# A four-stage mixer network on one core: constant products at four more places of TensorE's order, and the depthwise taps prepared later

## The chip, the cores and the metric

The kernel runs on 1 core of one Trainium2 chip. The metric is the device time of one execution in microseconds (us). Engines are named as the profile names them: PE is TensorE (matmuls), PEld its weight loads, DVE VectorE, ACT ScalarE, POOL GpSimd, SP the queue that issues the DMAs.

## The reference, cut to what matters

The input `x` is 16 images of 64 channels and 16 by 16 pixels, in single precision: 4096 tokens of 64 channels. Four stages follow one another, each a "conv" part and an "ffn" part with a residual:

```
x = x + _L0_conv_ref(_ln_c(x), ...)   # normed pixels -> 3x3 conv to 32 clusters, softmax, pooled, small MLP
t = t + _L0_ffn_ref(_ln_t(t), ...)    # router picks 127 of each image's 256 tokens, FFN 64->256->64
x = x + _L1_conv_ref(_ln_c(x), ...)   # four band means, argmax, two small products, sigmoid gate per image and channel
t = t + _L1_ffn_ref(_ln_t(t), ...)    # 16 experts 64->128->64, top 2, computed densely
x = x + _L2_conv_ref(_ln_c(x), ...)   # 3x3 depthwise conv, then linear attention with 8 heads
t = t + _L2_ffn_ref(_ln_t(t), ...)    # 8 experts 64->256->64, top 2, computed densely
x = x + _L3_conv_ref(_ln_c(x), ...)   # 3x3 conv 64->64 with weights quantised to 4 bits
t = t + _L3_ffn_ref(_ln_t(t), ...)    # 8 experts 64->128->64, the top 2 of each image
```

The comments are mine. In the first conv part the pixels are centred, scaled to unit length and convolved:

```
xn = l2norm(feature, axis=1)
sa = jax.nn.softmax(conv2d(xn, conv_up_w, conv_up_b, 1), axis=1)
```

In the second one the input is multiplied by a sigmoid gate `s` (`return x * s[:, :, None, None]`) that follows from band means through an argmax and two small products. The third one begins with `kdw = lax.conv_general_dilated(fmap, wdw, ..., feature_group_count=C)`: nine taps per channel.

## The kernel before

The whole of `x` stays on the chip. Tokens lie on the 128 partitions, in 32 tiles of 64 channels (`X`). The work goes through in G = 4 groups of 8 tiles (`TG`), or in 8 chunks of 512 tokens (`NCHUNK`). Each engine has one list of instructions, written out by hand at the end of `build`: for PE the order is `xt_tensor`, `w0_tensor`, `c0_tensor`, `u_tensor`, `t_tensor`, `f_tensor`, `v_tensor`, `e1_tensor`, `d_tensor` and so on, and for DVE `c0_vector`, `u_vector`, `t_vector`, `f_weights`, `f_vector`, `v_vector`, `e1_vector`, `d_vector`. An engine runs its list strictly in that order; between engines there are only semaphores (`wait_ge`, `then_inc`). What stands earlier in a list therefore delays all that stands behind it on that engine.

`keep_clock(pe, bank, count, tile)` (L421) issues `count` products of a constant 128 by 128 tile with itself into a PSUM bank that nobody reads; in single precision each shows as two MATMUL records. It stands in many gaps of PE's list.

The places that the change touches, in order of time:

- `w0_tensor` (L444) transposes the small weights of the first stage and then issues 6 constant products. Behind it, `c0_tensor` (L752) transposes the first group's unit-length pixels as soon as DVE has made them (L766, DVE L686); ACT copies them into the padded image (L722); the first convolution (`conv`, L784) is 72 records of 64 by 32 weights. After each convolution come two constant products and then the transposes of the logits (L799).
- `f_tensor` (L1174) is the first FFN. Its last loop turn, g == G, only transposes the last group's output back (`back`, L1242), which waits until DVE has consumed an earlier one (`f_yb`).
- `v_tensor` (L1351) computes band means (L1369), each group behind 6 constant products and a wait for the normed tokens, then 6 more constant products (L1373), the product for the argmax (L1374), the transposes of later weights (`prep_tensor`), 4 constant products, two small products (L1381, L1383), and last the gates: 16 products of 64 rows with a broadcast weight (L1388), a semaphore after every fourth.
- `e1_tensor` (L1783) begins with a wait for the second gated group (`x3`), 18 constant products, and then the transposes of group 0 (L609), which wait for DVE's `split` (L603, L604).
- DVE's `v_vector` (L1299) begins with `prep_taps` (L1643): two copies of the identity (L1648), four small instructions, and 18 `tensor_scalar` of 128x64 that place nine taps in a high and a low part (L1654, L1655). Behind them DVE copies the band means (L1307) that PE's L1374 waits for. After the argmax and `hq` (L1322) come `prep_vector` and `e1_weights_vector` (L1547), and then the gates' use (L1332). The taps are read only by the depthwise convolution in `d_tensor` (L2101).
- `e1_vector` (L1689) runs 16 experts over each chunk. For each expert e: `gate` (L1712) multiplies two hidden halves; PE's hidden products of expert e + 2 wait for it. At e % 4 == 3 two pair sums are weighed (`weigh`, L1717), which POOL adds up (L1500); the last two pairs of a chunk are weighed in the next chunk at e == 3, and PE transposes the finished sum at e == 6 (`experts_back`, L1589). At e == 7 and 8 the sum is reduced and added to X, at e == 9 to 13 the next layer norm's statistics are taken.

## Time and profile before

| | us |
|---|---|
| median of 3 runs | 706.9 |
| lowest, highest of the runs | 706.47, 711.89 |
| the profiled execution's own time | 704.68 |
| its span, first to last instruction | 702.9 |
| PE busy in it | 623.2 (89%) |
| DVE, ACT, POOL busy | 450.8, 364.4, 260.5 |
| mean granted clock of PE | 0.949 |

A clock of 1.00 is full speed, 0.50 the lower of the two levels. PE's busy time contains the constant products, so it says nothing by itself about what bounds the kernel; the chain of waits does. Times within the span count from its first instruction.

### The profile page before, as it was taken

How to read it: one execution, taken by the hardware profiler on the slowest of the kernel's cores; microseconds unless marked ns; L12 is line 12 of the kernel's file. 1: busy time of each engine (PE TensorE's matmuls, PEld its weight loads, DVE VectorE, ACT ScalarE, POOL GpSimd, SP SyncE). 2: the span in 40 equal slices, each digit the busy share in tenths (PEclk: the TensorE clock that was granted, in tenths of full speed). 3: DMA queues.
4: the chain of work that ended last, by engine and by line, in shares of the span. 5: the costliest groups of instructions: out<-in, count | busy, mean ns of one | idle time of the engine just before them, and what ended most of it. 6: DMA issues, size and time to landing. Idle time of an engine off the chain costs nothing.

```text
span 702.9 us, 12272 instructions
## 1 busy us (share of the span) xinstructions
PE 623.2 (89%) x3776; PEld 412.3 (59%) x3776; DVE 450.8 (64%) x1323; ACT 364.4 (52%) x777; POOL 260.5 (37%) x349
## 2 busy tenths in 40 slices
PE   7887788886999999999998998998999999996784
PEld 5675437774555555555556776895545445465652
DVE  6555797878777787778776477565433333438566
ACT  3234586176544444444436454455666777435375
POOL 6402555250653543444353000270333333335153
PEclk8999998798999999999999899989999999999897
DMA  4900000204343433524301000022222222100001
GB/s 110 159 6 1 2 0 1 61 2 101 87 112 76 97 83 68 113 61 112 68 9 30 1 2 0 1 51 52 77 70 80 60 61 61 31 2 0 2 2 60
DMA packets 24532, 34.62 MB, mean 49 GB/s; under 512 B 10984, under 2 KB 20224, under 8 KB 22368
## 3 DMA queue, kind: packets, MB, share of 16 engines
q1 hardware_dynamic: 24480, 33.95, 20.8%
q8 instruction: 30, 0.49, 0.3%
q14 instruction: 22, 0.18, 0.1%
HBM read 32.50 MB, written 1.44 MB: 48 GB/s over the span
## 4 chain that ended last, share of the span: by engine, by line
PE 61%; DVE 24%; ACT 6%; issue 4%; POOL 3%; DMA 1%; DVEq 1%; ACTq 0%; SPq 0%; POOLq 0%
PE ps L1808 13%; PE ps L2384 9%; PE ps L2400 8%; PE ps L1828 6%; DVE ST L492 3%; PE ps L2506 2%; PE ps L426 2%; PE ps L784 2%; PE ps L609 1%; PE ps L2782 1%; PE ps L1589 1%; PE ps L2111 1%; PE ps L2089 1%; PE ps L2113 1%; DVE tk L1106 1%
## 5 line engine op out<-in xcount | busy, mean ns | idle before, releaser
L1500 POOL TENSOR_TENSOR out_acc<-out_acc,tok_tmp 128x512 f32<-128x512 f32 x80 | 103.6, 1295 | 211.3 <-DVE tok_tmp L1717 114.7
L1808 PE MATMUL ps<-tokT,w 128*128 128x512 f32 x512 | 134.5, 409 | 3.4 <-DVE hid_buf L1712 1.9
L1769 ACT ACTIVATE act_buf<-ps 128x512 f32<-128x512 f32 x128 | 75.8, 596 | 92.0 <-PE ps L1808 88.4
L1808 PEld LDWEIGHTS ps<-tokT,w 128*128 128x128 f32 x512 | 92.6, 190 | 52.6 <-issue 24.3
L2384 PE MATMUL ps<-tokT,w 128*128 128x512 f32 x256 | 67.7, 406 | 1.5 <-ACT hid_buf L2357 1.5
L2384 PEld LDWEIGHTS ps<-tokT,w 128*128 128x128 f32 x256 | 45.4, 188 | 28.4 <-ACT hid_buf L2357 13.9
L426 PE MATMUL ps<-ones 128*128 128x128 f32 x416 | 58.4, 294 | 1.4 <-DVE X L1005 1.4
L1712 DVE TENSOR_TENSOR hid_buf<-act_buf,ps 128x512 f32<-128x512 f32 x64 | 43.5, 685 | 19.9 <-ACT act_buf L1769 16.3
L426 PEld LDWEIGHTS ps<-ones 128*128 128x128 f32 x416 | 53.6, 206 | 3.9 <-DVE X L1005 1.7
L1712 DVE TENSOR_TENSOR tok_split<-act_buf,ps 128x512 f32<-128x512 f32 x64 | 43.4, 686 | 15.7 <-ACT act_buf L1769 14.7
L537 ACT ACTIVATE U<-X,nmr,rstd 128x64 f32<-128x64 f32 x104 | 36.5, 430 | 23.4 <-POOL nmr L515 18.3
L2357 ACT ACTIVATE hid_buf<-ps,b 128x512 f32<-128x512 f32 x64 | 38.5, 682 | 17.3 <-PE ps L2384 17.3
L2357 ACT ACTIVATE tok_split<-ps,b 128x512 f32<-128x512 f32 x64 | 38.8, 690 | 13.1 <-PE ps L2384 12.8
L2313 DVE SCALAR_TENSOR_TENSOR tok_tmp<-ps,b,disp_all 128x512 f32<-128x512 f32 x24 | 18.0, 752 | 42.8 <-PE ps L2400 42.5
L1717 DVE TENSOR_TENSOR tok_tmp<-ps,disp_all 128x512 f32<-128x512 f32 x56 | 37.3, 688 | 6.4 <-PE ps L1828 3.5
L575 ACT ACTIVATE U<-X,nmr,rstd (+1 forms) x64 | 23.0, 430 | 25.6 <-POOL nmr L568 25.6
L514 POOL TENSOR_TENSOR rstd<-vpe,neghalf 128x8 f32<-128x8 f32 x20 | 34.4, 1721 | 1.7
L512 POOL TENSOR_TENSOR nmean<-mean2x,neghalf 128x8 f32<-128x8 f32 x20 | 4.7, 233 | 74.5 <-DVE var L499 74.3
L1828 PE MATMUL ps<-tok_split,w 128*64 128x512 f32 x128 | 31.0, 605 | 0.4 <-DVE tok_tmp L1717 0.4
L1828 PE MATMUL ps<-hid_buf,w 128*64 128x512 f32 x128 | 31.0, 605 | 0.0
L2400 PE MATMUL ps<-hid_buf,w 128*64 128x512 f32 x128 | 31.0, 605 | 0.0
L2400 PE MATMUL ps<-tok_split,w 128*64 128x512 f32 x128 | 30.9, 604 | 0.0
(475 smaller groups left out, 1133.7 us busy)
## 6 DMA issues: line engine op xcount, KB each, us to landing
disp_all<-disp_dram SPq DMA_DIRECT2D x32, 512.0 KB, 6.1
disp_all<-disp_dram SPq DMA_DIRECT2D x32, 256.0 KB, 3.9
w_raw<-in_L_ffn_w SPq DMA_DIRECT2D x4, 512.0 KB, 7.8
XIN<-in_x SPq DMA_DIRECT2D x4, 256.0 KB, 3.8
w_raw<-in_L_ffn_W SPq DMA_DIRECT2D x2, 512.0 KB, 5.8
out<-XIN SPq DMA_DIRECT2D x4, 256.0 KB, 2.2
fc_raw<-in_L_conv_upfc_w SPq DMA_DIRECT2D x1, 512.0 KB, 4.6
w<-in_L_ffn_w SPq DMA_DIRECT2D x1, 512.0 KB, 11.6
```

What stands on the lines that cost most here:

```text
L426: pe.matmul(ps[:, bank, 0:P], tile[:, :], tile[:, :], start=True, stop=True)
L514: plink(pool.tensor_tensor(rstd[:, t0:t1_], vpe[:, t0:t1_], neghalf[:, t0:t1_], ALU.pow))
L537: last = act.activation(U[:, tt, :] if dst is None else dst[:, t, :], src[:, tt, :], ACT.Identity, bias=nmr[:, tt:tt + 1], scale=rstd[:, t ...
L1500: pool.tensor_tensor(out_acc[:, :], out_acc[:, :], weighed[p % 2], ALU.add).then_inc(mm["acc"].sem, 1)
L1712: dve.tensor_tensor(hid_buf[e % 8][:, :], act_buf[e % 2][:, :], ps[:, 2 + e % 2, :], ALU.mult).then_inc(mm["m1"].sem, 1)
L1717: dve.tensor_tensor(out_acc[:, :] if p == 0 else weighed[p % 2], ps[:, 4 + p % 2, :], disp_all[:, p // 4, p % 4, :], ALU.mult).then_inc(mm ...
L1769: act.activation(act_buf[e % 2][:, :], ps[:, e % 2, :], ACT.Silu).then_inc(mm["act"].sem, 1)
L1808: last = pe.matmul(ps[:, 2 * k + e % 2, :], w12[:, part, k, EXPERT1[e], :], tokT[:, bass.ts(i, CHUNK)], start=(part == 0), stop=(part == 1))
L1828: last = pe.matmul(ps[f * C:(f + 1) * C, 4 + p % 2, :], w3[:, EXPERT1[e], :], hid_buf[e % 8][:, :], start=True, stop=True)
L2357: act.activation(hid_buf[u % 8][:, :], ps[:, u % 4, :], ACT.Gelu, bias=b1_6[:, unit:unit + 1]).then_inc(mm["act"].sem, 1)
L2384: last = pe.matmul(ps[:, u % 4, :], w1_6[:, part, e, h * P:(h + 1) * P], tokT[:, bass.ts(i, CHUNK)], start=(part == 0), stop=(part == 1))
L2400: last = pe.matmul(ps[r * C:(r + 1) * C, 4 + p % 2, :], w2_6[:, EXPERT2[u], h, :], hid_buf[u % 8][:, :], start=(h == 0), stop=(h == 1))
```

## The change

Five edits. (1) The constant products behind the first stage's weight transposes go from 6 to 11. (2) Two constant products are issued between the unit transposes and the first group's convolution. (3) In the last turn of the first FFN's loop PE waits for the last GELU (`f_h`) and issues 8 constant products into bank 3, ahead of the last `back`. (4) Behind each of the four groups of gates stand 3 constant products. (5) `prep_taps` leaves the head of `v_vector`; its six small instructions run in the experts' second chunk (`chunk(1, 0)`) at e == 3, ahead of `weigh`, and the 18 `tensor_scalar` are dealt out there as two behind each of the experts 4 to 12 (`place_tap`). In the added turn the code says `e == 3` and `4 <= e < 13`; nothing else in that chunk changes.

```diff
--- before.py
+++ after.py
@@ -454,7 +454,7 @@
             pe.transpose(ps[0:C, 1, C:2 * C], t1_raw[:, C:2 * C], ident[0:C, 0:C])
             pe.transpose(ps[0:C, 1, 2 * C:3 * C], t2_raw[:, :], ident[0:C, 0:C])
             pe.transpose(ps[0:C, 1, 3 * C:3 * C + K0], cent_raw[:, :], ident[0:K0, 0:K0]).then_inc(s_t[0], 1)
-            keep_clock(pe, 2, 6, ident)
+            keep_clock(pe, 2, 11, ident)
 
         def fc_tensor(pe):
 
@@ -769,6 +769,8 @@
             def conv(g):
 
                 xp = padded_pair[g % 2][:, :, :].rearrange("p q (y x) -> p q y x", x=PADW)
+                if g == 0:
+                    keep_clock(pe, 2, 2, ident)
                 pe.wait_ge(*m["c0_xp"](g + 1))
                 if g >= 1:
                     pe.wait_ge(*m["c0_cv"](g))
@@ -1255,6 +1257,9 @@
                     last.then_inc(m["f_mt_ps"].sem, 1)
                 if g < G:
                     outp(g)
+                if g == G:
+                    pe.wait_ge(*m["f_h"](2 * NCHUNK))
+                    keep_clock(pe, 3, 8)
                 if g >= 1:
                     back(g - 1)
 
@@ -1298,7 +1303,6 @@
 
         def v_vector(dve):
 
-            prep_taps(dve)
             dve.wait_ge(*m["v_w_ps"](1))
             dve.tensor_copy(l1w1T[:, :], ps[0:C, 7, 64:96])
             dve.tensor_copy(l1w2T[:, :], ps[0:C // 2, 7, 128:192]).then_inc(m["v_w"].sem, 1)
@@ -1389,6 +1393,7 @@
                                  ident[0:C, 0:C], start=True, stop=True)
                 if b % BG == BG - 1:
                     last.then_inc(m["v_sb_ps"].sem, 1)
+                    keep_clock(pe, 3, 3)
 
 
         def router_tensor(pe, g, w2, ne, bank, done):
@@ -1650,9 +1655,11 @@
             vlink(dve.tensor_copy(gw2_6[:, 0, :], gw_6[:, :]))
             dve.tensor_tensor(gw2_6[:, 1, :], gw_6[:, :], gw2_6[:, 0, :].bitcast(F32), ALU.subtract)
             vlink(dve.tensor_tensor(dw_lo[:, :], dw_raw[:, :], dw_hi[:, :].bitcast(F32), ALU.subtract))
-            for t in range(9):
-                dve.tensor_scalar(wdw[:, t, 0, :], ident2[:, :], dw_hi[:, t:t + 1].bitcast(F32), None, ALU.mult)
-                dve.tensor_scalar(wdw[:, t, 1, :], ident2[:, :], dw_lo[:, t:t + 1], None, ALU.mult)
+
+        def place_tap(dve, t):
+
+            dve.tensor_scalar(wdw[:, t, 0, :], ident2[:, :], dw_hi[:, t:t + 1].bitcast(F32), None, ALU.mult)
+            dve.tensor_scalar(wdw[:, t, 1, :], ident2[:, :], dw_lo[:, t:t + 1], None, ALU.mult)
 
         def prep_vector(dve):
 
@@ -1717,7 +1724,7 @@
                 dve.tensor_tensor(out_acc[:, :] if p == 0 else weighed[p % 2], ps[:, 4 + p % 2, :],
                                   disp_all[:, p // 4, p % 4, :], ALU.mult).then_inc(mm["w"].sem, 1)
 
-            def chunk(i, prev):
+            def chunk(i, prev, taps=False):
                 for e in range(E1):
                     gate(i, e)
                     if prev is not None:
@@ -1729,6 +1736,11 @@
                             dve.wait_ge(*mm["x"](prev + 1))
                         for step in STEPS_AT.get(e, ()):
                             chunk_stats(dve, prev, X, m["d_var"], step)
+                    if taps:
+                        if e == 3:
+                            prep_taps(dve)
+                        elif 4 <= e < 13:
+                            place_tap(dve, e - 4)
                     if e % 4 == 3:
                         for p in (e // 2 - 3, e // 2 - 2):
                             if p >= 0:
@@ -1738,7 +1750,7 @@
                     if prev is None:
                         router_top2(dve, mm, route1, 1, E1, e)
             chunk(0, None)
-            chunk(1, 0)
+            chunk(1, 0, taps=True)
             with vchain.loop(2, NCHUNK, 3) as i:
                 chunk(i, i - 1)
             for p in (PAIRS1 - 2, PAIRS1 - 1):
```

## Rows read from the trace of the kernel before

**Rows 1.** The page's span, and PE's clock in 40 slices

```profile
span 702.9 us, 12272 instructions
...
PEclk8999998798999999999999899989999999999897
```

**Rows 2.** Busy time by stretch, 12 to 22 us: length, five engines, clock, DMA share, GB/s

```profile
12.00:14.00 2.00, 0.67 (x6) 0.44 (x6) 1.93 (x13) 0.60 (x1) 2.00 (x1) 0.80 0.30 63
...
20.00:22.00 2.00, 1.31 (x31) 0.95 (x37) 1.54 (x3) 0.60 (x1) 0.51 (x1) 1.00 0.11 20
```

**Rows 3.** Instructions of PE by time, 1.5 to 24 us: start, us, what, idle before

```profile
1.57 2.50 PE L426 MATMUL ps<-ident 128*128 128x128 f32 x10 [1.57 <-POOL ident L408]
...
8.82 1.60 PE L426 MATMUL ps<-ident 128*128 128x128 f32 x12
12.55 0.66 PE L766 MATMUL ps<-ident,unit 128*128 128x128 f32 x4 [2.13 <-DVE unit L686]
13.99 4.49 PE L784 MATMUL ps<-padded_pair,w_cu_t 64*32 64x256 f32 x72 [0.78 <-ACT padded_pair L722]
...
21.48 2.36 PE L784 MATMUL ps<-padded_pair,w_cu_t 64*32 64x256 f32 x72 [0.69 <-ACT padded_pair L722]
```

**Rows 4.** The same of PE, behind the first FFN

```profile
107.06 1.09 PE L1242 MATMUL ps<-ident,ffn_outT 128*128 128x128 f32 x4 [2.91 <-DVE XIN L1117]
...
108.48 2.93 PE L426 MATMUL ps<-ones 128*128 128x128 f32 x12
```

**Rows 5.** Instructions of DVE by time: the last group of the FFN, and the taps

```profile
112.96 0.69 DVE L1117 TENSOR_TENSOR XIN<-ps,wm 128x512 f32<-128x512 f32 x1
...
120.62 0.39 DVE L1648 COPY ident<-ident 64x64 f32<-64x64 f32 x2 [0.61 <-ACT U L537]
...
121.58 0.25 DVE L1654 TENSOR_SCALAR wdw<-ident,dw_hi 128x64 fp32r<-128x64 f32 x1
...
124.35 0.25 DVE L1655 TENSOR_SCALAR wdw<-ident,dw_lo 128x64 fp32r<-128x64 f32 x1
...
124.74 0.20 DVE L1307 COPY ori<-ps 64x64 f32<-64x64 f32 x1
```

**Rows 6.** Instructions of PE by time, band means to the experts' transposes

```profile
121.97 1.60 PE L426 MATMUL ps<-ones 128*128 128x128 f32 x12
125.00 0.33 PE L1374 MATMUL ps<-ori,wencb 64*64 64x64 f32 x2 [1.42 <-DVE ori L1307]
...
129.24 7.08 PE L1388 MATMUL ps<-ident,sg 64*128 64x64 f32 x32 [0.27 <-ACT sg L1347]
136.25 5.81 PE L426 MATMUL ps<-ones 128*128 128x128 f32 x36
142.80 1.09 PE L609 MATMUL ps<-ident,tok_split 128*128 128x128 f32 x8 [0.74 <-DVE tok_split L604]
```

**Rows 7.** Busy time by stretch, where the gates begin

```profile
129.00:129.50 0.50, 0.26 (x1) 0.27 (x2) 0.49 (x3) 0.18 (x1) 0.00 (x0) 0.74 0.00 0
```

**Rows 8.** Instructions of DVE by time, around the first gated group

```profile
130.95 0.18 DVE L1547 TENSOR_TENSOR gw<-gw,gw 128x16 fp32r<-128x16 f32 x1
131.24 0.69 DVE L1332 TENSOR_TENSOR tok_tmp<-U,ps 128x512 f32<-128x512 f32 x1
...
134.60 0.69 DVE L1332 TENSOR_TENSOR tok_tmp<-U,ps 128x512 f32<-128x512 f32 x1
```

**Rows 9.** Instructions of DVE in the second chunk, behind expert 3, and at 8 and 12

```profile
191.38 0.69 DVE L1717 TENSOR_TENSOR tok_tmp<-ps,disp_all 128x512 f32<-128x512 f32 x1 [0.16 <-PE ps L1828]
...
200.25 0.69 DVE L1712 TENSOR_TENSOR hid_buf<-act_buf,ps 128x512 f32<-128x512 f32 x1 [0.52 <-ACT act_buf L1769]
...
206.04 0.69 DVE L1712 TENSOR_TENSOR tok_split<-act_buf,ps 128x512 f32<-128x512 f32 x1 [0.37 <-ACT act_buf L1769]
```

**Rows 10.** PE in the second chunk: the sum's transposes

```profile
195.45 0.66 PE L1589 MATMUL ps<-ident,out_acc 128*128 128x128 f32 x4 [0.26 <-POOL out_acc L1500]
```

**Rows 11.** ACT at the second chunk's end: the norm of the first chunk's tokens

```profile
209.96 1.44 ACT L575 ACTIVATE U<-X,nmr,rstd 128x64 f32<-128x64 f32 x4 [1.16 <-POOL nmr L568]
```

## The prediction

> **What bounds the kernel now.** The page's span and clock line come first [rows 1]: 702.9 us, of which two slices of 17.6 us stand at 0.7 of the clock; everywhere else it is nearly full. The chain of waits then says who sets the end where the change acts: from 12 to 24 us it runs over PE, ACT and DVE in turn, with the first convolution whole in it; from 102 to 147 us it is nearly all DVE, with short pieces of PE; from 170 us on it is PE in the experts. The order by time and the busy time by stretch give the prices.
>
> In the first stage PE waits 2.13 us for DVE's unit pixels and 0.78 us for ACT's copy [rows 3]. In that gap the granted clock falls: 0.80 over 12 to 14 us (full, then half), and 1.00 again from 20 us [rows 2]. The same 72 records take 4.49 us for the first group and 2.36 us for the second [rows 3]. Behind the FFN PE is idle for 2.91 us while DVE works [rows 4]. At 120.62 DVE starts on the taps and at 124.74 it copies the band means; PE has long finished its constant products and waits 1.42 us for that copy [rows 5, 6]. The gates run at half clock, 7.08 us for 32 records [rows 6, 7], though DVE takes each group when it comes to it. In the second chunk PE waits only 0.26 us for the sum [rows 10], and DVE has little left over [rows 9].
>
> **The prices of a constant product.** Twelve records (six products) took 1.60 us at full clock [rows 3, 6] and 2.93 us at half clock [rows 4]: 0.27 and 0.49 us a product.
>
> **Edits 1 and 2, the first convolution.** Five more products end at 10.42 + 1.35 = 11.8 us, before the unit transposes at 12.55; two more fit between the transposes' end (13.21) and the convolution (13.99): 0.54 us of 0.78. At full clock both cost nothing, since DVE and then ACT end those waits. At half clock the second pair would cost 0.98 - 0.78 = 0.2 us and the first five up to 11 x 0.49 - (12.55 - 8.82) = 1.7 us. The first ten records of the span took 2.50 us, the slow price, so the clock begins low, and the twelve from 8.82 took the fast one [rows 3]. The idle time left is 0.75 + 0.24 us instead of 2.13 + 0.78. If the clock stays up, the convolution takes 2.36 instead of 4.49 us (2.1 us), and the products and transposes behind it, at two levels in the rows of this stretch, give another 0.3 us. PE, ACT and DVE of groups 1 to 3 follow from that, and POOL's powers are ready ahead of them, so I take 2.4 us as kept to the end. Bounds: 0 (the clock falls all the same, or had not fallen) to 2.4.
>
> **Edit 3, behind the FFN.** The wait asks for the count that the last `outp`, ahead of it in PE's list, has waited for already, so it is free; queued behind it are the last `back` and the small transposes of `v_tensor`, which nobody waits for yet. Eight products are 2.1 us at full clock, inside the 2.91 us gap; at half clock 3.9 us, 1.0 too many. But DVE takes that `back` only at 112.96 [rows 5], 4.8 us after it ended [rows 4], so cover remains either way. DVE, POOL and ACT set the end until 120.5; PE's speed from 105 to 112 us gives back nothing. Price 0, bounds 0 to 0.
>
> **Edit 5, what it removes.** The 24 instructions stand from 120.62 to about 124.5 us, the 18 `tensor_scalar` (the first and the last are shown) 0.163 us apart [rows 5]. Without them the copy can run at 122.1, when the last band product is done. But PE has six constant products in its order ahead of L1374; they end at 121.97 + 1.60 = 123.57 [rows 6]. So L1374 moves from 125.00 to about 123.5: 1.5 us gained, not 3.9. All behind it (argmax, gates, X) moves with it.
>
> **Edit 5, what it adds.** At expert 3 of the second chunk the six small instructions take 121.58 - 120.62 = 0.96 us [rows 5], in front of the weighing at 191.38, for which DVE had been free for 0.16 us [rows 9]: 0.8 us later. POOL's last two sums follow, and PE, which already waits for them [rows 10], starts the transposes 0.8 us later. Behind the experts 8 to 11 four pairs cost 4 x 0.326 = 1.30 us on a DVE that from 200.25 to 206.04 shows 0.37 us of idle time [rows 9]; gate 12 comes 0.9 us late at most, and PE's second product of expert 14 waits for that gate. The last statistics and POOL's power come as much later, and then ACT's four norms, which already end a wait of 1.16 us and stand ahead of the third chunk's first Silu [rows 11]. PE has a few tenths in hand at each. Bounds 0 to 0.9 + 0.9 = 1.8 us, taken 0.85, the middle, since PE's double buffers take some of it once. Together 1.65 us. The pairs behind 4 to 7 fall into waits for ACT like that of 0.52 us ahead of gate 8 [rows 9] and cost nothing; if that cover were gone they would add 1.3 us. The taps' reader stands a whole stage further on, so nobody waits for them.
>
> **Edit 4, the gates.** At full clock a group of gates would come after 1.0 instead of 2.0 us. But DVE is in its own list until 131.13 and takes the first group at 131.24 [rows 8]: 0.1 us to gain. DVE takes the second group 3.36 us after the first [rows 8]; with three products each the groups come every 2.0 + 1.2 = 3.2 us at half clock, every 1.8 us at full clock. Then 18 products stand ahead of the transposes L609.
>
> **Sum**, against the profiled execution's own 704.68 us: - 2.4 - 1.5 - 0.1 + 1.65 = - 2.35, thus 702.3. The median of the runs lies 2.2 us above that execution, and I carry this over: 704.5 us.
>
> **Rival A: the convolution's clock is not there to be won.** In the gap before L784 the clock fell in this execution; one execution cannot say that it always does, and the runs of this one program spread from 706.47 to 711.89. If it had not fallen in the timed runs, or falls still, edits 1 and 2 give 0: 706.9 + 0.05 = 706.9. The Trainium skill (TensorE: Matmul & The Clock Gate, Part 1) says that the gate's look at PE is not tied to the kernel's start and that the transition varies from run to run. By that rule A would hold in part of the executions; the sum above takes the fall as seen. No row of one execution can show it.
>
> **Rival B: slower, by the gates.** The clock falls where the gates begin, as it did at 129 us [rows 7]. With a thin mixture of gates and constants it stays at 0.50 through all four groups: 7.08 us, plus 24 records x 0.24 = 5.9, thus 13.0 us, and then the 18 products, which took 5.81 us in part at half clock [rows 6]. From 127.7 that ends at 146.5 us, where DVE's split has been ready since about 141.3 (142.8 - 1.5): 5.2 us late, straight on the path. This decides once the clock is still low when the third group ends. The total would be 706.9 - 2.35 + 5.2 = 709.8. For it: the clock stayed at 0.50 for all 32 records before. Against it: constants at half clock brought it up within the row of 36 that followed.
>
> **Rival C: the taps are free.** PE hides the whole of edit 5's addition, as its short waits in the second chunk allow [rows 10]: 704.5 - 1.65 = 702.9.
>
> **How the numbers follow.** Forecast 0.37; A 0.33; B 0.15; C 0.12; 0.03 for something else. The likeliest gives 704.5 us. With 0.6 us for other executions on both sides, the range from C's 702.9 less that and some of the unshown to B's lower part is 701.8 to 708.8; it leaves out the upper half of B and little below. About 1% (7 us) is what a measurement of this kernel can tell from no change. Faster than 699.8 would need every bound and more: 0.04. Slower than 714.0 would need B and a second wait: 0.03. The rest, 0.93, is the same.
>
> **What would show it.** Right: the first convolution's 72 records in 2.4 us; L1374 about 1.5 us after the last band product, with no wait for DVE; the transposes L1589 of the second chunk behind a wait of about 1 us; a gap of some tenths on PE near the third chunk's start. Wrong: half clock in that convolution (A), constants of the gates still running when DVE's first split is done (B), no longer waits of PE in the second chunk (C). A range missed below would mean that the clock was low in places that this trace shows high.

## The result: slower by 0.9%, where no change was forecast

The changed kernel took 713.41 us (median of 20 runs, 706.59 to 718.49), the kernel before 706.36 us on the same chips (20 runs, 702.05 to 711.89). The ratio is 1.0088, 95% interval 1.0064 to 1.0112. The forecast was 704.5 us, 701.8 to 708.8. Ratios here and below leave out runs over 1.5% above the fastest of the same kernel; where that matters, the mean of all runs is given beside it.

The profiled execution of the changed kernel took 715.96 us, that of before 704.68 us: 11.3 us to explain. The page has the span, and PE's clock in slices of 17.9 us. Two slices stand at 0.6 now, from 107 to 143 us, where there was a 0.7 and a 0.8 [rows 1].

```profile
span 714.2 us, 12380 instructions
...
PEclk9998996688999999999999899968999999999997
```

The first convolution came as forecast. In the order by time (start, duration, what, idle before and its releaser) its 72 records take 2.36 us instead of 4.49 us [rows 3]; the products ahead of it end in time.

```profile
13.98 2.36 PE L786 MATMUL ps<-padded_pair,w_cu_t 64*32 64x256 f32 x72 [0.34 <-ACT padded_pair L722]
```

Behind the FFN it goes wrong. The same view, 102 to 127 us:

```profile
102.35 1.95 PE L426 MATMUL ps<-ones 128*128 128x128 f32 x16
105.42 0.63 PE L1244 MATMUL ps<-ident,ffn_outT 128*128 128x128 f32 x4 [1.13 <-DVE XIN L1119]
...
106.29 1.60 PE L426 MATMUL ps<-ones 128*128 128x128 f32 x12
110.02 1.39 PE L1373 MATMUL ps<-band,U 128*64 128x4 f32 x16 [2.13 <-ACT U L537]
111.33 2.93 PE L426 MATMUL ps<-ones 128*128 128x128 f32 x12
114.19 1.87 PE L1373 MATMUL ps<-band,U 128*64 128x4 f32 x16
115.99 2.93 PE L426 MATMUL ps<-ones 128*128 128x128 f32 x12
...
120.65 2.93 PE L426 MATMUL ps<-ones 128*128 128x128 f32 x12
...
126.41 0.32 PE L1378 MATMUL ps<-ori,wencb 64*64 64x64 f32 x2
```

With edit 3's eight products at 102.35 the clock is full here, and everything after them is over early: the six constants at 106.29 take 1.60 us where before they took 2.93 us [rows 4]. PE then idles for 2.13 us, and while the first band means run the clock falls. From there each group costs 4.66 us (111.33 to 115.99 to 120.65): six constants at half clock and 16 records of band means at half clock. ACT delivers a group every 3.4 us, so no group waits any more and PE falls behind. The encoder's product L1378 stands at 126.41; without its taps DVE does nothing but wait for it:

```profile
124.98 0.22 DVE L1311 COPY ori<-ps 64x64 f32<-64x64 f32 x1 [5.78 <-PE ps L1373]
```

At the gates (order by time of PE, then of DVE):

```profile
130.65 1.57 PE L1392 MATMUL ps<-ident,sg 64*128 64x64 f32 x8 [0.27 <-ACT sg L1351]
132.15 1.65 PE L426 MATMUL ps<-ones 128*128 128x128 f32 x6
133.73 1.97 PE L1392 MATMUL ps<-ident,sg 64*128 64x64 f32 x8
...
140.67 1.97 PE L1392 MATMUL ps<-ident,sg 64*128 64x64 f32 x8
142.57 7.61 PE L426 MATMUL ps<-ones 128*128 128x128 f32 x42
150.02 1.04 PE L609 MATMUL ps<-ident,tok_split 128*128 128x128 f32 x8
```

```profile
143.10 0.72 DVE L604 TENSOR_TENSOR tok_split<-U,tok_split 128x512 fp32r<-128x512 f32 x1
```

DVE's split is ready at 143.82 us, PE comes to it at 150.02: 6.2 us late, behind 21 constants in a row. The busy time by stretch (length, five engines, clock, DMA share, GB/s) shows the three long stretches at half clock. PE had no idle time in any of them:

```profile
111.00:124.00 13.00, 13.00 (x77) 12.28 (x76) 4.72 (x23) 7.83 (x21) 4.62 (x8) 0.50 0.00 0
132.00:148.00 16.00, 16.00 (x69) 14.86 (x69) 14.97 (x67) 5.52 (x16) 8.11 (x15) 0.50 0.33 66
470.00:486.00 16.00, 16.00 (x76) 15.65 (x75) 6.35 (x27) 6.84 (x15) 8.62 (x11) 0.50 0.29 55
```

The third lies in the second experts' router, code that the change doesn't touch. Before, half clock lasted there from 463.7 to 470.5 us. In the second chunk, DVE's weighing comes at 198.00 (191.38 [rows 9]) and ACT's norm at 218.38 (209.96 [rows 11]); the six small instructions stand ahead of the first, and a pair of `tensor_scalar` behind each expert. Two of these pairs, the ones behind the experts 4 and 8, fall together with work of POOL and take much longer than the others (DVE's order by time, with POOL's row beside it):

```profile
198.00 1.29 DVE L1724 TENSOR_TENSOR tok_tmp<-ps,disp_all 128x512 f32<-128x512 f32 x2
...
200.75 1.31 DVE L1662 TENSOR_SCALAR wdw<-ident,dw_lo 128x64 fp32r<-128x64 f32 x1
...
208.25 0.72 DVE L1661 TENSOR_SCALAR wdw<-ident,dw_hi 128x64 fp32r<-128x64 f32 x1
```

```profile
208.01 0.91 POOL L1582 TENSOR_TENSOR w<-w_whole,w 128x256 fp32r<-128x256 f32 x1
```

```profile
218.38 1.44 ACT L575 ACTIVATE U<-X,nmr,rstd 128x64 f32<-128x64 f32 x4 [1.80 <-POOL nmr L568]
```

**Where the 11.3 us arose in this execution**, by starts against those of before: L1378 +1.4, L609 +7.2, the first weighing of the second chunk +5.9 (174.09 to 179.96; part of PE's lateness meets waits that were there), ACT's norm +8.4. The half clock of 17 instead of 7 us in the later router brings 4.4 more, and a shorter stretch near 670 us takes 1.5 back.

### The profile page after: what moved, and what is told of

Read it like the earlier page. It is cut to its first block, busy times and chain, and to the rows that moved or that the text cites. A ratio compares the mean times of both kernels' runs of the same rounds, so it can differ in the third digit from the quotient of the medians.

```text
span 714.2 us, 12380 instructions
## 1 busy us (share of the span) xinstructions
PE 639.6 (90%) x3830; PEld 429.1 (60%) x3830; DVE 452.0 (63%) x1323; ACT 364.3 (51%) x777; POOL 260.3 (36%) x349
## 3 DMA queue, kind: packets, MB, share of 16 engines
q1 hardware_dynamic: 24480, 33.95, 20.4%
## 4 chain that ended last, share of the span: by engine, by line
PE 48%; DVE 13%; ACT 3%; issue 3%; POOL 2%; DVEq 1%; ACTq 0%; POOLq 0%
PE ps L1820 11%; PE ps L2396 8%; PE ps L2412 8%; PE ps L1840 5%; PE ps L2518 2%; DVE ST L492 1%; PE ps L609 1%; PE ps L2123 1%; PE ps L2101 1%; PE ps L1594 1%; PE ps L2125 1%; PE ps L2113 1%; PE ps L2144 1%; PE ps L2794 1%; DVE U L592 1%
## 5 line engine op out<-in xcount | busy, mean ns | idle before, releaser
L426 PE MATMUL ps<-ones 128*128 128x128 f32 x456 | 71.2, 315 | 0.8 <-DVE X L1007 0.8
L426 PEld LDWEIGHTS ps<-ones 128*128 128x128 f32 x456 | 65.2, 225 | 3.6 <-DVE X L1007 1.1
```

What stands on the lines that cost most here:

```text
L426: pe.matmul(ps[:, bank, 0:P], tile[:, :], tile[:, :], start=True, stop=True)
```

## The experiments

Each was run 12 times unless said otherwise, those of one group on one chip together with the kernel before. The theory: constants in PE's fixed order cost what they take at half clock wherever PE has no wait left to put them in; this happens at the band means and at the gates. The rivals: edit 5's addition costs it, or the clock falls by chance alone. A ratio has an interval of about 0.3% to either side, so the difference of two ratios is known to about 0.4%.

**First group: each edit alone** (before: 706.88 us). Edit 5 alone, the taps moved and nothing else:

```diff
-            prep_taps(dve)
...
-            chunk(1, 0)
+            chunk(1, 0, taps=True)
```

> Edit 5 alone: the taps leave the head of v_vector and go into the experts' second chunk; no constant product is added. Theory 1 (constant products in PE's fixed order decide): the profile shows 2.5 us more between the second chunk's expert 3 and the third chunk's start, as in the changed kernel, and 0 to 1.5 us less at L1374, because six constant products stand ahead of it; time +1.0 to +2.5 us against before. Theory 2 (the chunk's DVE work is the main cost): +4 us or more.

Measured 708.93 us, ratio 1.0025 [0.9994, 1.0055]. The trace has both halves. The encoder's product stands at 122.48, 2.5 us earlier than before; 1.0 of this was there already at the last `back` (106.03, 107.06 before [rows 4]), where edit 5 has not acted yet, so the taps' removal gave 1.5 us. And the distance to before, -2.8 us at the second chunk's start, is -0.3 us at its end.

```profile
106.03 1.00 PE L1242 MATMUL ps<-ident,ffn_outT 128*128 128x128 f32 x4 [2.91 <-DVE XIN L1117]
...
122.48 0.33 PE L1373 MATMUL ps<-ori,wencb 64*64 64x64 f32 x2
```

Edit 4 alone:

```diff
                     last.then_inc(m["v_sb_ps"].sem, 1)
+                    keep_clock(pe, 3, 3)
```

> Edit 4 alone: three constant products behind each group of gates. Theory 1: where the clock is low at the gates it stays low through all four groups, PE's list is 24 records of 0.22 us = 5.3 us longer there, 0.7 us of it covered, and the first transposes L609 come 4 to 5 us late, straight on the path: +3 to +5 us, the largest of the single edits. Theory 2: the clock is up sooner and the products lie in PE's spare time: 0 us, -1 at best.

Measured 710.16 us, ratio 1.0055 [1.0028, 1.0081]. The order by time of PE has the 21 constants and the late transposes, with the band means undisturbed:

```profile
140.47 6.34 PE L426 MATMUL ps<-ones 128*128 128x128 f32 x42
146.65 1.04 PE L609 MATMUL ps<-ident,tok_split 128*128 128x128 f32 x8
```

Edit 3 alone:

```diff
+                if g == G:
+                    pe.wait_ge(*m["f_h"](2 * NCHUNK))
+                    keep_clock(pe, 3, 8)
```

> Edit 3 alone: eight constant products in the gap behind the first FFN. Theory 1: the clock is up for the constants that follow, PE is through with them early and idles ahead of the first band means, and the clock falls just there; four groups of 12 slow constants and 16 slow band records take 4.7 us each against the 3.4 us in which the tokens come, and L1374 is up to 2 us late: 0 to +2 us. Theory 2: a higher clock can only help: -1 to 0 us.

Measured 708.02 us, ratio 1.0044 [1.0009, 1.0080]. Its one profiled execution took only 704.18 us, the lowest of its 12 runs: there PE waits the same 2.13 us and the clock stays up.

```profile
112.43 1.09 PE L1372 MATMUL ps<-band,U 128*64 128x4 f32 x16 [2.13 <-ACT U L537]
113.46 1.60 PE L426 MATMUL ps<-ones 128*128 128x128 f32 x12
```

Edits 1 and 2 alone:

```diff
-            keep_clock(pe, 2, 6, ident)
+            keep_clock(pe, 2, 11, ident)
...
+                if g == 0:
+                    keep_clock(pe, 2, 2, ident)
```

> Edits 1 and 2 alone: constants ahead of the first convolution. All theories: the 72 records take 2.36 us in the profile. If the fall of the clock there was usual, -2.4 us; if it came in part of the executions only, -1 us; if its gain is given back later by the clock, 0.

Measured 708.63 us, ratio 0.9997 [0.9964, 1.0030]. The median says more than the ratio because the runs lie in two heaps, five from 701.9 to 704.8 us and seven from 708.3 to 710.4. The profile shows the convolution in 2.36 us and then, from 54.7 us, half clock for 6.8 us instead of 3.4, and for 17 us in the later router. The four ratios multiply to +1.2%, the whole measured +0.9%. By the means of all runs (two of over 1000 us left out) the four are 1.0021, 1.0047, 1.0024 and 1.0002, together +0.9%, as is the whole (1.0094). So the single losses add up, and nothing in the time asks for edits that make one another worse.

**Second group: parts left out** (before: 704.98 us). The changed kernel without edit 4:

```diff
                     last.then_inc(m["v_sb_ps"].sem, 1)
-                    keep_clock(pe, 3, 3)
```

> The changed kernel without edit 4 (no constants between the gates). Theory 1 (the constants in PE's fixed order decide, those of the gates most): the first split of the experts' tokens is transposed within 1 us of being ready, where the changed kernel needed 6.2 us; 3.5 to 5 us are given back: +0.2 to +0.5% against before. Theory 2 (the chunk's DVE work decides): no difference to the changed kernel, +0.9%.

Measured 707.70 us, ratio 1.0035 [1.0004, 1.0067]. The band means run at half clock exactly as in the changed kernel, L1378 at 125.69, but the transposes again wait for DVE:

```profile
110.81 2.93 PE L426 MATMUL ps<-ones 128*128 128x128 f32 x12
113.67 1.87 PE L1373 MATMUL ps<-band,U 128*64 128x4 f32 x16
...
125.69 0.33 PE L1378 MATMUL ps<-ori,wencb 64*64 64x64 f32 x2
...
143.10 1.09 PE L609 MATMUL ps<-ident,tok_split 128*128 128x128 f32 x8 [0.34 <-DVE tok_split L604]
```

Without edits 3 and 4:

```diff
-                if g == G:
-                    pe.wait_ge(*m["f_h"](2 * NCHUNK))
-                    keep_clock(pe, 3, 8)
...
-                    keep_clock(pe, 3, 3)
```

> Edits 1, 2 and 5 alone. The single edits measured 0.9997 and 1.0025. If they add, 1.000 to 1.003. If the constants of edit 3 are needed by the moved taps (the band means at full clock), it is above 1.004.

Measured 704.41 us, ratio 0.9990 [0.9964, 1.0016] (mean of all runs 1.0012): the loss is in edits 3 and 4, and 1, 2 and 5 together give nothing that can be told from none.

The changed kernel with 6 instead of 18 constants ahead of the experts' transposes:

```diff
             pe.wait_ge(*m["x3"](2))
-            keep_clock(pe, 3, 18)
+            keep_clock(pe, 3, 6)
```

> The changed kernel with 6 instead of 18 constants ahead of the experts' first transposes. Theory 1 (what PE is late by there is its own list): 12 products of 0.44 us are gone where the clock is low, the first transposes L609 come within 1 us of the split; 3 to 5 us less than the changed kernel, +0.2 to +0.5% against before. A rival (the constants are what brings the clock up for the transposes and the router behind them; without them these run at half clock): 0 to 2 us less than the changed kernel.

Measured 706.79 us, ratio 1.0035 [1.0005, 1.0065]. PE reaches L609 4.1 us earlier (145.94), 2.7 us behind the split, and the transposes then run at half clock (1.74 us instead of 1.04). By the ratios more than half of the loss goes with those constants, at the edge of what their intervals can tell; the profiled execution doesn't show it, since at 715.06 us it was the slowest of the 12.

A version of my own: edits 1 and 2, the taps in DVE's wait for POOL before the last norm (five pairs) and behind experts 4 to 7 (four pairs), two instead of six constants ahead of the encoder's product (against the kernel before, edits 1 and 2 not shown):

```diff
+            prep_taps(dve)
+            for t in range(5):
+                place_tap(dve, t)
             ln_norm_vector(dve, G - 1, m["v_rstd"], m["v_u"])
...
+                    if taps and 4 <= e < 8:
+                        place_tap(dve, e + 1)
...
             last.then_inc(m["v_ori_ps"].sem, 1)
-            keep_clock(pe, 3, 6)
+            keep_clock(pe, 3, 2)
```

> A version built on theory 1: edits 1 and 2; no edit 3 or 4; the taps' small instructions and five of the nine pairs in DVE's 2.7 us wait for POOL ahead of the last band means, the other four pairs behind the experts 4 to 7 of the second chunk; and 2 instead of 6 constants ahead of L1374. Theory 1: L1374 comes 2.5 us earlier, the second chunk costs nothing more: -2.5 us, with the first convolution's share up to -4.5 us (-0.3 to -0.6%). Theory 2 (any DVE work in the second chunk costs it): +1 us back.

Measured 704.89 us, ratio 1.0010 [0.9975, 1.0044]. In the trace the encoder's product stands at 120.86 and L609 at 138.23, 4.6 us ahead of before; 17.1 us at half clock from 457 us give most of it back.

**Third group: the gap and the addition** (before: 706.14 us). Eight more constants that fill PE's wait in front of the band means:

```diff
                 if b % BG == 0:
-                    keep_clock(pe, 3, 6)
+                    keep_clock(pe, 3, 14 if b == 0 else 6)
```

> The changed kernel with eight more constant products in front of the first group's band means, which fill the wait of 2.13 us that PE has there. Theory 1 (the idle gap of 2.13 us in front of the first band means is what lets the clock fall at 110.6 us): no gap, the clock stays at full, the groups take 1.60 us for twelve constants instead of 2.93 us, the encoder's product starts near 121 to 122.5 us; the gates at half clock remain as they are. Profiled execution about 4 us shorter than the changed kernel's, ratio to before 1.003 to 1.007. Rival (the load of the constants is too thin or the look falls elsewhere; the clock falls all the same): the eight are eight more records at half clock, 2 us later still, the product near 128 us, ratio 1.010 or more.

Measured 708.05 us, ratio 1.0017 [0.9988, 1.0046], against 1.0088 for the changed kernel. PE's order by time:

```profile
105.55 3.39 PE L426 MATMUL ps<-ones 128*128 128x128 f32 x28
109.28 1.09 PE L1373 MATMUL ps<-band,U 128*64 128x4 f32 x16 [0.34 <-ACT U L537]
110.31 1.60 PE L426 MATMUL ps<-ones 128*128 128x128 f32 x12
...
121.14 0.32 PE L1378 MATMUL ps<-ori,wencb 64*64 64x64 f32 x2
...
136.34 6.98 PE L426 MATMUL ps<-ones 128*128 128x128 f32 x42
143.16 1.04 PE L609 MATMUL ps<-ident,tok_split 128*128 128x128 f32 x8
```

With the wait down to 0.34 us the clock holds, L1378 comes at 121.14 instead of 126.41, and the gates still hold the transposes: the split was ready at 138.45, 4.7 us before. The rival that the clock falls all the same is out for this execution, and the ratio says that it is out for most: the difference of 0.7% is larger than its uncertainty.

The changed kernel without edit 3 alone (edit 4 stays):

> The changed kernel without edit 3 (no constants behind the first FFN); edits 1, 2, 4 and 5 stay. Theory 1 (each place where constants stand in PE's order decides by itself): the band means run at full clock again, since the six constants of the first group bring the clock up before them as in the profile of before; the product with the encoder's weights (L1374 of before) starts near 122.5 us instead of 126.41 us; the gates still hold PE late, DVE's split is ready at about 140 us and PE comes to its transposes near 146 us. Profiled execution 4 to 6 us shorter than the changed kernel's 715.96 us; ratio to the kernel before 1.003 to 1.007. Theory 2 (edit 3 is harmless, the gates alone cost): ratio as the changed kernel's, 1.009. Theory 3 (edit 3 carries all of it): 0.999 as without edits 3 and 4.

Measured 711.94 us, ratio 1.0081 [1.0051, 1.0110], above my 1.003 to 1.007. Its profiled execution (705.26 us, the lowest of its 12 runs) has the band means at full clock and L609 4.7 us behind the split, as expected. But by the ratio nothing was given back: this is what Theory 2 said (the mean of all runs, 1.0066, is the upper end of Theory 1's range). It is also just what edits 4 and 5 alone add up to, 0.55% and 0.25%. Whether the band means ran at half clock in the other 11 runs no trace says; that they can without edit 3 the next run shows.

Edit 5's addition without its removal:

```diff
+            for t in range(9):
+                place_tap(dve, t)
...
-            chunk(1, 0)
+            chunk(1, 0, taps=True)
```

> The kernel before, with the taps prepared where they were and a second time in the experts' second chunk (at expert 3 and behind experts 4 to 12): edit 5's addition without its removal; the values are the same. My forecast's price for the addition: 1.65 us, bounds 0 and 2.6. The trace of the changed kernel showed the distance to the kernel before growing by 2.5 us over this chunk. Theory 1: the distance grows by 2.2 to 2.7 us between 190 and 215 us, in two steps (expert 3, and experts 8 to 12), ratio 1.002 to 1.004. Rival (PE's buffers absorb the second step as I forecast): 1.65 us or less, ratio 1.000 to 1.002.

Measured 708.04 us, ratio 1.0018 [0.9987, 1.0048]. DVE's weighing and ACT's norm:

```profile
178.62 0.69 DVE L1721 TENSOR_TENSOR out_acc<-ps,disp_all 128x512 f32<-128x512 f32 x1 [1.60 <-DMA disp_all<-disp_dram]
...
196.61 1.29 DVE L1721 TENSOR_TENSOR tok_tmp<-ps,disp_all 128x512 f32<-128x512 f32 x2
```

```profile
217.02 1.44 ACT L575 ACTIVATE U<-X,nmr,rstd 128x64 f32<-128x64 f32 x4 [1.85 <-POOL nmr L568]
```

The distance to before is 4.53 us at the chunk's first weighing, 5.23 at the third pair's and 7.06 at the norm: 0.7 us for expert 3, 1.8 us for experts 8 to 12, together 2.5 us. In the changed kernel it is 5.87, 6.62 and 8.42, again 2.5. (The two pairs that fall together with POOL's work are as long here: 1.30 us for one `tensor_scalar` behind expert 4, 0.73 us for one behind expert 8.) And this trace, whose code up to here is that of before, has the band means at half clock through all four groups:

```profile
109.48 2.93 PE L426 MATMUL ps<-ones 128*128 128x128 f32 x12
...
114.45 2.93 PE L426 MATMUL ps<-ones 128*128 128x128 f32 x12
...
129.37 0.32 PE L1376 MATMUL ps<-ori,wencb 64*64 64x64 f32 x2
```

The encoder's product stands at 129.37 instead of 125.00 [rows 6]; 1.0 us of this was there at the last `back` (108.05), 3.4 us arose behind it, although DVE's taps were in place.

My version plus two constants in PE's wait of 0.70 us in the later router (461 us before):

```diff
-                if g:
-                    keep_clock(pe, 2, 3)
+                keep_clock(pe, 2, 3 if g else 2)
```

> The version with edits 1 and 2, the taps' preparation in DVE's wait for POOL and in experts 4 to 7 of the second chunk, two constants in front of the encoder's product, and new: two constant products in PE's wait of 0.70 us ahead of the second group's transposes of the second experts' router (461 us in the profile of before). Theory 1 (the 17 us at half clock that this stage shows in some executions begin in that wait): the stretch is 6.8 us or absent, the profile some 4 us shorter than the version's own 702.4 us, ratio 0.994 to 0.997. Rival (the many small products with one column that surround the wait let the clock fall, filled or not): half clock for 6.8 or 17 us as before, ratio 0.998 to 1.002.

Measured 704.04 us; ratio 0.9917 [0.9872, 0.9961]. It was run nine times, and the runs spread from 697.02 to 709.12 us; by the mean of all nine the ratio is 0.9950. The profile has the 17 us at half clock all the same.

**Fourth group** (before: 705.55 us). A second trace of the changed kernel, one run:

> The changed kernel once more, for a second trace of the same code. Theory 1 (with the gap of 2.13 us in front of the band means the clock falls in some executions and not in others, by where the looks fall): the stretches at half clock begin at other places, the band means may be at full clock (groups of 1.60 us, encoder's product near 122.5 us) or at half (2.93 us, near 126.4 us). Theory 2 (the gap makes it fall always): again 2.93 us and about 126 us. The gates: half clock in all four groups, L609 of the first group at 144 to 150 us by both.

It took 708.96 us. The clock fell behind the same wait, and one row of constants takes 2.93 us instead of three:

```profile
108.85 1.09 PE L1373 MATMUL ps<-band,U 128*64 128x4 f32 x16 [2.13 <-ACT U L537]
109.88 2.31 PE L426 MATMUL ps<-ones 128*128 128x128 f32 x12
...
114.03 2.93 PE L426 MATMUL ps<-ones 128*128 128x128 f32 x12
...
122.24 0.32 PE L1378 MATMUL ps<-ori,wencb 64*64 64x64 f32 x2
...
144.26 1.04 PE L609 MATMUL ps<-ident,tok_split 128*128 128x128 f32 x8
```

The version with the eight constants, without edit 4:

> The changed kernel with eight more constants in front of the band means and without edit 4 (no constants between the gates). Theory 1 (the loss is PE's constants at half clock at two places, and both are taken away): DVE's split sets the first transposes of the experts' router again, near 139.5 us instead of 143.16 us with edit 4; profiled execution 3 to 4 us shorter than the 705.7 us of the version with the eight, ratio to the kernel before 0.996 to 0.999. Rival (the gates' share is not on the path in the timed runs): ratio as with edit 4, 1.002.

Measured 703.67 us (701.23 to 706.06), ratio 0.9957 [0.9928, 0.9986]; the mean of all 12 runs gives 0.9956. It is faster than both kernels. PE's order by time at the gates:

```profile
121.85 0.32 PE L1378 MATMUL ps<-ori,wencb 64*64 64x64 f32 x2
...
126.09 5.72 PE L1392 MATMUL ps<-ident,sg 64*128 64x64 f32 x32 [0.27 <-ACT sg L1351]
132.81 6.66 PE L426 MATMUL ps<-ones 128*128 128x128 f32 x36 [0.99 <-DVE X L1337]
139.31 1.04 PE L609 MATMUL ps<-ident,tok_split 128*128 128x128 f32 x8
```

PE waits 0.99 us for DVE before its 18 constants, and takes the split (ready at 139.17) 0.1 us after it is there.

My version with and without the two constants of the later router, side by side:

> The version with edits 1 and 2, the taps' preparation and five pairs in DVE's wait for POOL, four pairs in the second chunk, two constants in front of the encoder's product: once more, beside the next one on the same chip. If its gain of 4.6 us by 138 us holds in most executions, ratio 0.994 to 0.998; if half clock elsewhere gives it back as in its first timing (1.001), 1.000.

> The same with two constants in PE's wait of 0.70 us in the later router. Theory 1 (its first ratio, 0.9917, came from the two constants): 0.99 to 0.995, and at least 0.003 below the version without them. Rival (its profile showed 17.1 us at half clock there all the same, so the two constants do nothing, and the ratio was the luck of nine runs): within 0.003 of the version without them.

Measured 707.19 us and 703.65 us, ratios 0.9969 [0.9930, 1.0009] and 0.9885 [0.9847, 0.9923]; by the means of all 12 runs 0.9991 and 0.9942. The trace of the first has the band means at half clock for all four groups (L1378 at 125.08), that of the second has not.

**Fifth group** (before: 706.72 us). The two constants on top of the version with the eight constants and without edit 4, and alone:

> Edits 1, 2, 3 and 5, no edit 4, eight more constants in front of the first band means (0.9957 before), and two constants in PE's wait of 0.70 us in the later router. Theory 1 (those two keep the clock up in part of the executions): half clock behind 457 us for 6.8 us or less in some executions, ratio 0.990 to 0.994. Rival (they do nothing): 0.9957 within 0.003.

> The kernel before with only the two constants in PE's wait of 0.70 us in the later router. Theory 1: 0.994 to 0.997. Rival (they do nothing, the two versions' spread was the early stages' own): 0.998 to 1.002.

Measured 703.85 us, ratio 0.9954 [0.9924, 0.9984], and 704.35 us, ratio 0.9978 [0.9940, 1.0016]. On top of the eight constants they change nothing. Alone, the trace shows no half clock there at all (and 10 us of it with them on top of the eight), while each of the 16 traces without the two constants has 6.8 to 23.9 us. In the two traces of my own version with them it lasted 17.1 us. What they do to the time is not shown: 0.9978 alone has 1 inside its interval, and the 0.9885 was no price to go by, since its 12 runs spread from 694.22 to 710.70 us.

## Why the prediction was wrong

Two steps failed: edit 4, taken as a gain of 0.1 us, cost about 4 us, and the price of 0 to 0 behind the first FFN left out that the clock can fall in the band means, about 5 us by the run that prevents it. A third was a size, 1.65 us for the taps' addition, where the traces have 2.5.

**Edits 1 and 2: right in the trace, not seen in the time.** "The convolution takes 2.36 instead of 4.49 us": it takes 2.36 us in each of the 14 traces with these edits. In the six without, it took 3.88 to 4.49 us, so my 4.49 was the upper end. Rival A's clock that is "not to be won" did not occur. But "kept to the end" failed: the last `back` comes at 105.16 us by the mean of the 14 traces and at 106.79 by that of the six, so 1.6 of 2.4 us are left there. In the changed kernel's own trace (105.42, 107.06 before [rows 4]) half clock lasts 6.8 instead of 3.4 us at 56 us. And the bound for five products at half clock came true in the trace of the version with the eight constants and the two of the later router: the unit transposes stand at 14.23 instead of 12.55 us, and the first reduction behind the convolution at 19.62, where it stands in four of the six traces without the edits (19.52 to 19.68). In 12 of the other 13 it stands near 18.0. Alone the edits measured 0.9997, whose interval just holds the whole 2.4 us. What they earn stays open.

**Edit 3 and the band means: a step that failed.** The text gave "Price 0, bounds 0 to 0", with the reason that "PE's speed from 105 to 112 us gives back nothing". It priced the products and not what can follow from their being quick. The six constants behind them had filled PE's wait because they ran at half clock (2.93 us, wait 0.24 us); at full clock they leave 2.13 us, and in four of five traces with edit 3 and no filling the clock falls in the band means, in three of them until the last group. With the wait filled it falls in none of three. From the last `back` to the encoder's product it takes 16.5 us where the clock holds and 21.0 us where it falls until the last group: 4.5 us. Filling the wait took 0.7% off the changed kernel and 0.8% off the version without edit 4 (1.0088 to 1.0017, 1.0035 to 0.9957), about 5 us, give or take 3. That filling the wait gives this time back is shown. That edit 3 brings the fall about is not: of twelve traces without edit 3 two have the fall through all four groups too (the one with the taps twice, and my version's second), and leaving edit 3 out gave back nothing that the ratio can show (1.0081). The ratios put its own share at 0.4% alone, 0.4% beside edit 5 (0.9990 to 1.0035) and 0.1% beside edits 4 and 5; the means of all runs say 0.2 to 0.3% in all three. How often and for how long the clock falls in the timed runs, no trace says.

**Edit 5's removal: right, and no more than that.** I took "L1374 moves from 125.00 to about 123.5", 1.5 us gained, with all groups at full clock. From the last `back` to this product it takes 17.9 us in the five traces with the taps on DVE and the clock up, and 16.5 us in the six without them: 1.5 us, as forecast. Where the clock falls for the whole stretch the taps make no difference: 21.3 us with them (the trace with the taps twice), 20.4 us in my version's second, which has four constants fewer there (0.9 us). So their place on DVE covers PE's lateness by 1.4 us, PE's wait at L1374 before [rows 6]; the rest is on the path either way. In the changed kernel this gain was lost with the fall, and DVE waits 5.78 us for the band means, where it waits 1.26 us with the eight constants.

**Edit 4: the step that cost most for certain; Rival B, at 0.15, was what happened.** The sum took "0.1 us to gain", with a group every "2.0 + 1.2 = 3.2 us at half clock", inside DVE's 3.36. Three products at half clock are 1.5 us by the forecast's own price, and the groups came every 3.47 us (133.73 to 137.20 to 140.67). Behind them stood 21 constants in a row, the first of them at half clock. Rival B's text has 5.2 us late at L609; the traces have 4.7 us (edit 4 alone, the second one of the changed kernel, the one without edit 3, the one with the eight constants) and 6.2 us in the profiled execution. Its condition, "once the clock is still low when the third group ends", held in every trace with the gates' constants. The reason that I set against it, that the clock had come up within a row of constants before, spoke of 18 in a row and not of three between gates. Here too it came up only within the row behind the last gates. In time it cost 0.55% alone, 0.53% beside edits 3 and 5, 0.60% with the band means at full clock (1.0017 to 0.9957): 3.7 to 4.2 us, three times about the same.

**Edit 5's addition: under-sized.** 1.65 us forecast, 2.5 us in three traces (the changed kernel, edit 5 alone, taps twice). Expert 3 was right (0.8 forecast, 0.7), and so were the pairs behind 4 to 7, which cost nothing. "Bounds 0 to 0.9 + 0.9, taken 0.85, the middle, since PE's double buffers take some of it once": 1.8 us, the upper bound, is what it costs. The four pairs were priced at 0.326 us each, from a place where POOL was idle. Of the 1.8 us, 1.1 arise at expert 8 alone, between gate 8 (6.60 us behind before) and gate 9 (7.74): there POOL is at work, the first `tensor_scalar` takes 0.72 us instead of 0.24, and the addition to X ahead of it 0.88 instead of 0.54. Each `tensor_scalar` that begins while POOL is at work there ends within 0.1 us of POOL's instruction, in all three traces (by POOL's spans, which are rough). What in the two engines' work causes this is not shown. ACT waits 1.80 us for POOL instead of 1.16.

**The sum.** Forecast for the profiled execution 702.3 us, measured 715.96: 13.7 more. By starts (121.1 forecast for L1378, 126.41 measured), 5.3 up to the encoder's product (0.8 of the first gain lost, 4.5 band means); 4.6 for the gates (5.9 at L609, less 1.3 that met waits); 0.9 in the second chunk; 2.9 behind it, in code that is the same. The range ended at 708.8 us, below Rival B's own 709.8; for two places at once it had no room at all, and for the band means no case, since they had "bounds 0 to 0".

## What to carry to other kernels

Constants that keep the clock up are free only inside a wait. Where PE has none they cost their price at the clock that they meet, here three times about 4 us for twelve products at half clock, and they pay only if they bring the clock up before the work that is on the path. When an edit makes PE's earlier work faster, the wait behind it grows by as much: look at that wait too, and fill it, as the eight constants did. A cover is worth its length and no more: the taps on DVE hid 1.4 us of PE's lateness, not the 4.5 us of the fall. And a price that was read where the other engines were idle need not hold beside their work.

## What the runs showed of the hardware

Behind a wait of 2.13 us, with PE at full clock before it, the clock fell in four of five traces; with 0.34 us of wait in its place it fell in none of three. Once it had fallen, 13.00 us of PE without any idle time passed at 0.50 in the band means and 16.00 us at the gates; at the gates, with or without constants between them, it rose in no trace before the row of constants behind the last group.

A `tensor_scalar` of 128x64 on DVE took 0.24 us with POOL idle. Where it began while POOL was at an elementwise product or sum it took 0.32 to 1.31 us and ended with POOL's instruction (three traces).

The same code shows half clock in the later router for 6.8 us in one trace and 23.9 us in another, and the runs of the kernel before spread by some 10 us; with the wait filled and without the gates' constants they spread by 4.8 us. The Trainium skill (TensorE: Matmul & The Clock Gate, Part 1) says that the transition varies from run to run, which these traces bear out. It also puts the cost of the ramp under 1% of a typical span. That is more than one fall costs here, 4.5 us or 0.6% of the span in the band means, but in this kernel the clock falls many times, and these 4.5 us with the 4.4 us of the later router are together 1.2%; the mean granted clock of the profiled execution is 0.938.
